# Second attention of a four-batch transformer kernel: fp32 scores by rows and by columns instead of turned probabilities

## The reference, cut to what matters

```python
q = jnp.concatenate([q_p, q_r], axis=-1)      # 16 heads of 32 channels
k = jnp.concatenate([k_p, k_r], axis=-1)
scores = jnp.einsum('bqhd,bkhd->bhqk', q, k) * scale
scores = jnp.where(causal[None, None], scores, jnp.finfo(scores.dtype).min)
probs = jax.nn.softmax(scores, axis=-1)
out = jnp.einsum('bhqk,bkhd->bqhd', probs, v).reshape(b, s, H)
return out @ o_w
```

## Time and profile before

| | |
|---|---|
| median of 3 runs | 2114.62 us (2110.89 to 2117.39) |
| the profiled execution's own time | 2111.37 us |
| its span | 2109.2 us |
| PE busy in the span | 1872.0 us (89%) |
| DVE busy | 1377.6 us (65%) |
| ACT busy | 993.7 us (47%) |
| POOL busy | 785.0 us (37%) |
| mean granted clock of PE | 0.932 |

### The profile page before, as it was taken

One profiled execution on the slowest core, in us unless ns is written; L12 is line 12 of the kernel. 1 busy time (PEld: TensorE's weight loads), 2 busy tenths in 40 slices (PEclk: granted clock), 3 DMA queues, 4 the chain that ended last, 5 costly groups with the idle time before them and its releaser, 6 DMA issues. The chain is left out here.

```text
span 2109.2 us, 27324 instructions
## 1 busy us (share of the span) xinstructions
PE 1872.0 (89%) x9162; PEld 1225.7 (58%) x9162; DVE 1377.6 (65%) x2196; ACT 993.7 (47%) x1738; POOL 785.0 (37%) x1057
## 2 busy tenths in 40 slices
PE   7978665998999899898999899899899899899795
PEld 3446443695448565595447656497447666588342
DVE  5765699475663799576664599577654499667311
ACT  1412674362322797363232698264242498365031
POOL 1146277441210276471120167372110157472201
PEclk9989755999999999999999999999999999999898
DMA  6336200000213175210113076210022157210683
GB/s 255 116 114 225 76 0 21 1 2 1 100 46 120 45 264 190 90 32 21 74 57 120 30 245 229 90 41 21 35 96 90 55 197 267 105 41 21 260 293 104
DMA packets 55063, 221.03 MB, mean 105 GB/s; under 512 B 6288, under 2 KB 6288, under 8 KB 46992
## 3 DMA queue, kind: packets, MB, share of 16 engines
q1 hardware_dynamic: 45776, 195.19, 26.5%
q0 software_dynamic: 5120, 16.78, 2.4%
q10 hardware_dynamic: 4032, 7.34, 1.0%
HBM read 179.70 MB, written 39.58 MB: 104 GB/s over the span
## 5 line engine op out<-in xcount | busy, mean ns | idle before, releaser
L1953 POOL TENSOR_TENSOR Y<-Y,HC 128x1024 f32<-128x1024 f32 x116 | 273.7, 2361 | 174.6 <-DVE HC L1349 173.9
L1338 DVE TENSOR_TENSOR_SCAN HS<-DA,ps 128x1024 f32<-128x1024 f32 x128 | 292.3, 2284 | 23.9 <-PE ps L747 13.0
L1707 ACT ACTIVATE DA<-DL,AB,AN 128x511 f32<-128x511 f32 x256 | 193.9, 807 | 14.7 <-DVE HS L1338 13.5
L966 PE MATMUL ps<-ring,XBT 128*128 128x512 f32 x384 | 188.5, 597 | 0.0
L1821 ACT ACTIVATE PD<-ps,NMX 128x128 f32<-128x128 f32 (+3 forms) x256 | 134.9, 529 | 101.3 <-DVE NMX L1483 99.2
L537 PE MATMUL ps<-ring,XNT 128*128 128x512 f32 x384 | 175.5, 614 | 6.5 <-ACT VA L1654 4.3
L1483 DVE TENSOR_REDUCE NMX<-ps 128x1 f32<-128x128 f32 (+3 forms) x256 | 124.4, 487 | 65.1 <-PE ps L810 64.8
L828 PE MATMUL ps<-V,PTD 128*128 128x33 f32 x1280 | 164.2, 262 | 0.0
L828 PEld LDWEIGHTS ps<-V,PTD 128*128 128x128 f32 x1280 | 162.6, 192 | 0.5 <-ACT PTD L844 0.5
L655 PE MATMUL ps<-XNH,tern 128*128 128x512 f32 x352 | 140.4, 399 | 9.3 <-DVE tern L1238 5.3
L1349 DVE TENSOR_TENSOR HC<-HS,ps 128x1024 f32<-128x1024 f32 x120 | 143.3, 1196 | 0.0
(11 more groups left out here) (251 smaller groups left out, 4003.8 us busy)
## 6 DMA issues: line engine op xcount, KB each, us to landing
ring<-experts_dram SPq DMA_DIRECT2D x48, 1024.0 KB, 5.2
tern<-tern_q SPq DMA_DIRECT2D x33, 768.0 KB, 4.3
ring<-experts_dram SPq DMA_DIRECT2D x48, 512.0 KB, 5.6
RAW<-tern_dram SPq DMA_DIRECT2D x22, 768.0 KB, 4.8
ring<-wqkv_dram SPq DMA_DIRECT2D x4, 3072.0 KB, 11.8
XB<-xg SPq DMA_DIRECT2D x42, 256.0 KB, 3.8
yg<-YB SPq DMA_DIRECT2D x42, 256.0 KB, 5.0
tern_q<-tern SPq DMA_DIRECT2D x11, 768.0 KB, 7.0
```

Source lines behind the costliest of these rows:

```text
L966: last = pe.matmul(ps[:, g_bank(b)], XBT[:, b % 2, k], weights(b)[:, k * C:(k + 1) * C], start=(k == 0), stop=(k == NK - 1), skip_group_ch ...
L1338: v.tensor_tensor_scan(HS[:, q].rearrange("p j t -> p (j t)"), DA[:, q].rearrange("p j t -> p (j t)"), ps[:, 2 * q:2 * q + 2].rearrange("p ...
L1707: s.activation(DA[:, u % 2, jj, 1:T], DL[:, j, 1:T], ACT.Exp, scale=AN[:, j * NS + n:j * NS + n + 1], bias=AB[:, j * NS + n:j * NS + n + 1 ...
L1953: p.tensor_tensor(y, y, HC[:, q], ALU.add).then_inc(c_y, 1)
```

## The change

Stage D takes heads in pairs like stage A. The steps per pair:

- by rows: fp32 scores with queries on the partitions (`pe_D_rows`), contraction over 32 channels, two heads in two row groups, and the bf16 mask on the diagonal block of each. DVE takes the negated maxima of both heads at once (`v_D_max`) and ACT writes them as diagonal matrices in fp32r (`s_D_diag`, tile `DG`).
- by columns: the same scores with keys on the partitions (`pe_D_cols`), and onto each a product of a matrix of ones with the diagonal matrix, which adds to each column its query's negated maximum. ACT takes the exponential, POOL zeroes the masked part (`p_A_select`, as in stage A).
- the product with V as in stage A (`pe_pv`), in three pieces, and the normalisation as in stage A (`v_pair`), which writes the heads already transposed, into `AOTD`.

The splitting on POOL, the transposes of stacks, of probabilities and of heads, and their copies are gone. In their place queries and keys are transposed once per tile (`pe_qk`). The output projection is in two parts: the products over three quarters of the channels (`pe_project_part`) lie before and behind the last product with V, and the last quarter follows when the last pair is normalised. The gathers of the experts' rows stand on POOL ahead of the selects; two of them now wait for the first combined rows. The statistics and transposes of the next batch, the scaling of the residual and the tiles' places in memory move as well.

```diff
+            for t in range(NP + 2):
+                rows, cols, heads = t < NP, 1 <= t <= NP, t >= 2
+                if rows:
+                    pe_D_rows(pe, t, 0)
+                if cols:
+                    pe_D_cols(pe, t - 1, 0)
+                if t == NP + 1:
+                    for i in range(2):
+                        pe_project_part(pe, i)
+                if rows:
+                    pe_D_rows(pe, t, 1)
+                if heads:
+                    pe_D_pv(pe, t - 2, (0,))
+                if rows:
+                    pe_D_rows(pe, t, 2)
+                if cols:
+                    pe_D_cols(pe, t - 1, 1)
+                if heads:
+                    pe_D_pv(pe, t - 2, (1,))
+                if cols:
+                    pe_D_cols(pe, t - 1, 2)
+                if heads:
+                    pe_D_pv(pe, t - 2, (2, 3))
+                if t >= NP:
+                    for i in (2 * (t - NP), 2 * (t - NP) + 1):
+                        pe_norm(pe, 0, i)
+            for i in range(2, NT):
+                pe_project_part(pe, i)
             pe_project_D(pe)
...
+        def pe_D_rows(pe, p, unit):
+
+            if unit == 1:
+                if p >= 2:
+                    pe.wait_ge(a_exp, 3 * (NP + p - 1))
+            elif p or unit:
+                pe.wait_ge(d_max, max_count(p, 0) if unit else max_count(p - 1, 2))
+            bank = d_rows_bank(unit)
+            for i, off in D_ROWS[unit]:
+                n = (i + 1) * P
+                for x, (h, rows) in enumerate(heads_of(p)):
+                    pe.matmul(ps[:, bank + x, off:off + n], QT[rows, h // 4, tile(i)], KT[rows, h // 4, 0:n],
+                              start=True, stop=False, skip_group_check=True)
+                for x in range(2):
+                    last = pe.matmul(ps[:, bank + x, off + n - P:off + n], identb, mask_q, start=False, stop=True,
+                                     skip_group_check=True)
+            last.then_inc(d_scores, 1)
+
+        def pe_D_cols(pe, p, unit):
+            if unit == 0:
+                pe.wait_ge(d_diag, NT * (p + 1))
+                if p:
+                    pe.wait_ge(a_exp, 3 * (NP + p - 1) + 2)
+            elif unit == 1:
+                pe.wait_ge(a_exp, 3 * (NP + p) + 1)
+            else:
+                pe.wait_ge(d_max, max_count(p + 1, 1) if p + 1 < NP else NT * NP)
+                if p + 1 == NP:
+                    pe.wait_ge(a_exp, 3 * (NP + p))
+            bank = d_cols_bank(unit)
+            _, first, _ = A_UNIT[unit]
+            for kt in (k for k in range(NT) if A_PLACE[k][0] == unit):
+                off = A_PLACE[kt][1] - first
+                n = T - kt * P
+                for x, (h, rows) in enumerate(heads_of(p)):
+                    pe.matmul(ps[:, bank + x, off:off + n], KT[rows, h // 4, tile(kt)], QT[rows, h // 4, kt * P:T],
+                              start=True, stop=False, skip_group_check=True)
+                for x in range(2):
+                    last = pe.matmul(ps[:, bank + x, off:off + n], ONES[:].bitcast(F32R), DG[p % 2][:, x, kt * P:T],
+                                     start=False, stop=True, skip_group_check=True)
+            last.then_inc(a_scores, 1)
+
+        def pe_D_pv(pe, p, blocks):
+            if 0 in blocks:
+                if p == 0:
+                    pe.wait_ge(ones_a[1], 1)
+                pe.wait_ge(a_sel, NP + p + 1)
+                if p:
+                    pe.wait_ge(a_head, NP + p)
+            for kt in blocks:
+                last = pe_pv(pe, p, kt, 0)
...
+        D_ROWS = (((3, 0),), ((2, 0), (0, 3 * P)), ((1, 0),))
...
         def pe_project_D(pe):
 
+            pe.wait_ge(a_head, 2 * NP)
+            for i in range(NT):
+                pe.matmul(ps[:, 2 + i], AOTD[:, NK - 1, tile(i)], wo1[:, NK - 1], start=False, stop=True,
+                          skip_group_check=True).then_inc(proj_done, 1)
+            for i in range(NT):
+                pe_norm(pe, 4, i)
+
+        def pe_project_part(pe, i):
+            for k in range(NK - 1):
+                pe.matmul(ps[:, 2 + i], AOTD[:, k, tile(i)], wo1[:, k], start=(k == 0), stop=False,
+                          skip_group_check=True)
...
+            for t in range(NP + 3):
+                if t >= 3:
+                    v_pair(v, 1, t - 3)
+                if t < NP:
+                    for unit in range(3):
+                        v_D_max(v, t, unit)
+                if experts and 1 <= t <= NT:
+                    for n in (2 * t - 2, 2 * t - 1):
+                        v_combine(v, n)
...
+                if t in (7, 9):
+                    for i in (t - 7, t - 6):
+                        v_normalize(v, 0, i)
+                if t == 9:
+                    if experts:
+                        v.wait_ge(stored, 16)
+                    v.wait_ge(n_base, NT)
+                    for i in range(NT):
+                        v.tensor_scalar(ACC[:, i], X[:, i], MV[:, i, 0:1], RS[:, i, 1:2], ALU.subtract,
+                                        ALU.mult).then_inc(y_base, 1)
...
+            for t in range(NP + 1):
+                rows, cols = t < NP, t >= 1
+                if cols:
+                    s_D_exp(s, t - 1, 0)
+                if rows:
+                    s_D_diag(s, t, 0)
+                    s_D_diag(s, t, 1)
+                if cols:
+                    s_D_exp(s, t - 1, 1)
+                if rows:
+                    s_D_diag(s, t, 2)
+                if cols:
+                    s_D_exp(s, t - 1, 2)
+            for i in range(NT):
+                s_copy_bank(s, ("norm", 0, i), XNT[:, :, tile(i)])
...
+                    if n == 6:
+                        p.wait_ge(e_comb, 2)
+                    p_gather(p, n)
+            for n in range(NP):
+                p_A_select(p, NP + n)
```

More of the change, by code:

```diff
@@ L112 @@
           + [(("norm", 3, i), ("act", "dve")[i == NT - 1]) for i in range(NT)]
-          + list(d_transposes())
-          + [(("heads", 1, i), "act") for i in range(NT)]
+          + [(("qk2", i, z), ("act", "dve")[z]) for i in range(NT) for z in range(2)]
+          + [(("norm", 0, i), "act") for i in range(NT)]
           + [(("norm", 4, i), "act") for i in range(NT)])
@@ L492, in pe_norm @@
             last.then_inc(t_full, 1)
-        def pe_stack(pe, g, i):
-            pe.wait_ge(stack_ready, 2 * (NT * g + i + 1))
-            bank = t_bank(pe, ("stack", 1, g, i))
-            for j in range(2 * GH):
-                last = pe.transpose(ps[:, bank, tile(j)],
-                                    STK[:, i, j].rearrange("p a d -> p (a d)").bitcast(F32),
-                                    ident)
-            last.then_inc(t_full, 1)
         def pe_project_A(pe):
@@ L932, in pe_E_down @@
                 c = GU + m * C
-                last = pe.matmul(ps[:, e_down_bank(i)], GE[m][:, tile(i)], ring[:, 2, c:c + C],
+                last = pe.matmul(ps[:, e_down_bank(i)], ge(m)[:, tile(i)], ring[:, 2, c:c + C],
                                  start=(m == 0), stop=(m == 1))
@@ L1634, in s_A @@
             for p in range(NP):
+                if p == 1 and experts:
+                    xs_all_sent(s)
                 for unit, (_, col, width) in enumerate(A_UNIT):
```

349 lines of the change are left out of this document (116 added, 233 removed).

## The result

| | before | after |
|---|---|---|
| time, median of 4 runs each | 2113.05 us | 2437.95 us (2433.02 to 2442.79) |
| ratio, 95% interval | | 1.1535 [1.1504, 1.1566] |
| profiled execution: span | 2109.2 us | 2440.9 us |
| mean granted clock of the span | 0.932 | 0.814 |
| first stage D loop, first score to end of the last product with V | 84.1 us | 169.2 us |

The forecast was 2179 us with a range of 2128 to 2202. The sign was right and the size was far off: +325 us where +65 were forecast.

The account below looks back on a forecast made before the run. PE was taken to bound the stage D loop: 99.8 us against 84.1 (+15.7), tail +0.5, so +16.2 per batch and +65 over four, 2176 us, plus 3.2 for the median: 2179 us, range 2128 to 2202.

Parts of the forecast that it names:

- P: PE time per pair of heads in the stage D loop: scores, V, masks, ones and changes of form, 11.40 us.
- 8 P - R + 12.74: Stage D loop, first score to last product with V: 99.8 us, R being the 4.12 us by rows.
- t = 0: rows alone, with waits for the maxima: Loop's first step: row blocks without columns, PE waiting for DVE's maxima, 4.95 us.
- A change of form: PE switching array tiling: entering 32-row groups 0.20 us, exits to masks and ones 0.15, entries into V 0.10; 19 per pair.
- The ones: PE's fp32r products of ones with the diagonals, 8 per pair: 1.26 us, with 0.23 at 512 columns.
- The ring of waits: Loop chain from V through normalisation, first maximum and PE's following work to V: 10.5 us, 0.9 below P.
- rival 1: Half price: each change of form costs 0.10 us, P 10.2, total 2143 us; chance 0.17.
- rival 2: Changes of form nearly free: P 8.7 us, total 2098 us; chance 0.12, of it 0.09 faster.
- rival 3: DVE's ring binds, two-bank maximum 2.5 us, changes at full 0.20: P 12.1, about 2205 us; chance 0.09.
- Rival 4: Two heads do not run side by side in rows and columns: P 15.7, about 2308 us; chance 0.02.
- The projection and the tail: After the last V: first DVE tile later, then DVE at 3.4 us per tile instead of 3.87; in all +0.5 us.
- all exits at 0.20: Top of the range: every exit from 32-row groups to masks and ones costs 0.20 us instead of 0.15.

Follow-up runs that it names:

- e_filler: Changed kernel plus whole-array products into a free bank, four before the second attention loop's first step and six before its second; 2227.48 us.
- e_full: Changed kernel with every second-attention score product contracting over all 128 rows instead of the head's 32 (different output); 2235.90 us.
- g_best: Changed kernel with scores grouped (11 form changes per pair), accumulation start fixed, projection parts moved, two whole-array fillers per batch before the second step; 2108.70 us.
- g_best0: g_best without any filler; 2126.39 us, ratio to before 1.0054.
- e_kick: Changed kernel plus 16 whole-array products of 512 columns inserted at the loop's fourth step; 2310.67 us.
- e_fill1: Changed kernel plus one whole-array filler per batch before the second step's first scores; 2391 us in two runs, 2450 to 2455 in two.
- g_pairs: Changed kernel with scores grouped (11 form changes per pair), column scores reading the other pair's rows so at most two lie side by side; 2290.71 us.

## Why the prediction was wrong in size

**The step that failed: "The sum is P = 11.40 us per pair against 10.22 before", carried into the loop as 8 P - R + 12.74.** Its durations were all read at a granted clock of 1.00 and put into a loop of another shape. Neither the sum nor a rival asked whether the clock would stay; the prediction thought of a fall in the tail alone. In the loop it was at 0.50, and P measured 20.55 us. The four loops measure 169.2, 168.5, 164.0 and 171.4 us against 99.8 forecast, together 274 us, which is all of the 259 us missed and a little more; the tail gave some back. e_filler shows that the clock is the cause: with it held at 1.00, the first loop takes 105.0 us, of which its six fillers, 5.3 us less the 1.1 us of wait they cover, are 4.2. That leaves 100.8 against 99.8.

Why the clock falls is known in part. The first steps were in the working: "t = 0: rows alone, with waits for the maxima", at 4.95 us, and the profile has 408.07 - 403.04 = 5.03. I priced them as time alone. They can decide the level of the whole loop: whole-array work put there (e_filler) or whole-array scores (e_full) kept it at 1.00. The wait for the maxima itself is not the cause in general, since three of the four loops fell before it began. The Trainium skill has a rule that would have raised the question, in "TensorE: Matmul & The Clock Gate", section "HAM oscillation — how this bites in real kernels": in its example, waits of 3 to 5 us for DMA between short groups of matmuls put the clock back to its low level. It would not have forecast this fall: no wait here is longer than 1.13 us, and e_full and the kernel before have waits as long at 1.00. The same page's table of the two states has the high level follow from sustained work; the trace doesn't agree, since PE was busy 156.02 of 157.00 us at 0.50.

**A change of form, the price of a pair.** The sum was right where the clock was: P = 11.40 forecast, 11.40 measured at 1.00. That it is right to 0.01 is luck, since its parts were less so. 512 columns of scores take 452.67 - 451.61 = 1.06 instead of 0.86, and two masks 0.22 instead of 0.14. So an entry costs 0.10 + 0.08 = 0.18 (0.20 forecast) and an exit 0.10 (0.15 forecast). The ones were dearer: 454.61 - 453.95 = 0.66 with the entry's gap of 0.08 in it, 0.58 where 0.46 was forecast. The errors cancelled.

**The ring of waits and the other engines.** Right. The maximum of 1024 elements over two banks takes 1.23 us, as forecast, and PE does not wait for DVE's maxima after the second step begins. The rivals were sums at full clock, and e_filler answers them there: P was 11.4, not 10.2 (rival 1), 8.7 (rival 2) or 12.1 (rival 3). Rival 4 is out too: four records of 512 columns take 1.06 us, so the two heads lie side by side.

**The projection and the tail.** Forecast +0.5 us, measured about 1.3 us less than before. The loop's last two steps hold, as long as the clock does. The two-part projection by itself was not undone in any run.

**The range.** Its top end, 2202, was a sum at full clock. The working says "all exits at 0.20", but that alone gives P = 11.8 and about 2192; 2202 takes the entries into V at 0.20 as well. At half clock every term of the loop is worth almost double (20.55 / 11.40 = 1.80), and no case had that.

## What to carry over

When a long loop on PE is rebuilt, look at its first microseconds as closely as at its steady state: what PE does there can decide the clock of the 160 us behind it, and "PE 99% busy" does not say at which level. Read the granted clock beside the busy time for every loop, and where it is 0.50 with PE full, try a little whole-array work in the first steps before anything else is tuned: two fillers a batch, 7 us in all, were worth 17.7 us (g_best against g_best0). Do not take the longest wait in sight for the cause: put the moment at which the clock falls beside the moment of the wait, in every loop and not only the first. Where the level is at stake, more work can cost less time: e_full does more per pair and is 202 us shorter than the changed kernel.

## What the runs showed of the hardware that was not expected

- One instruction sequence can run at either level for 50 us and more with PE busy throughout: 11.4 us per pair at 1.00 and 20.5 at 0.50, in one loop of e_kick.
- The clock fell with PE busy throughout the 2.6 us before (970.59 to 973.20), on matmuls of 32 rows behind a stretch with waits of 0.35 to 0.92 us; with waits of the same size and whole-array scores it did not (e_full).
- Near the edge it is not the same from loop to loop: e_fill1 differs by 60 us between runs, g_pairs from batch to batch.
- A start of accumulation in one part of a bank also resets the other: with `start=True` on both blocks of a bank the additions to the first were lost, with `start=(off == 0)` they were not. The Trainium skill says so in "PSUM — Partial Sum Buffer", section "The four PSUM rules": the first matmul of a group clears the written bits of the whole 2 KiB bank.
